# The layer-norm transposes move from TensorE and PSUM to transposing DMAs on the sync engine's queue

## The reference

```
x = x + 0.5 * ffn(layernorm(x))
x = x + attn(layernorm(x))
x = x + 0.5 * ffn(layernorm(x))

attn: q, k, v = x@Wq+bq, x@Wk+bk, x@Wv+bv       # 16 query heads, 4 key/value heads, head size 64
      out = softmax(causal(q/8 @ k.T)) @ v
      out = layernorm(out)*ln_g + ln_b ; return out @ Wo + bo

ffn:  cluster_scores = x @ cluster_sigs.T ; tile_scores = x @ sigs.T     # 8 + 64 columns
      tile_idx = best of 8 tiles in the best of 8 clusters (spline-calibrated gates)
      comp = tanh(gelu(x@w1 + b1) @ w2 + b2)                             # 1024 -> 256 -> 2
      mag  = relu(comp @ spline_w1[tile_idx] + ...) @ spline_w2[tile_idx] + ...
      return layernorm(x + mag * directions[tile_idx] * output_scale) * gamma + beta
```

## Time and profile before

| | us |
|---|---|
| median of 9 runs | 1154.55 (1151.77 to 1174.88) |
| the profiled execution | 1154.83 |
| its span, slowest core (7) | 1153.3 |
| spans of the other cores | 1141.0 to 1148.3 |

### The profile page before, as it was taken

The page is one execution under the profiler, slowest core; times in us unless marked ns, Lnnn a source line. Parts: engine busy times, 40 slices in busy tenths (PEclk is TensorE's granted clock), DMA queues, the critical chain, the costliest instruction groups (busy, mean ns, idle before and its releaser), DMA issues.

```text
span 1153.3 us, 12663 instructions; the slowest of 8 cores (1141.0 to 1153.3 us)
## 1 busy us (share of the span) xinstructions
PE 809.7 (70%) x3804; PEld 322.3 (28%) x3804; DVE 482.8 (42%) x921; ACT 508.7 (44%) x489; POOL 14.2 (1%) x22
## 2 busy tenths in 40 slices
PE   2067663595999556757778878888469958766097
PEld 1043211233444312312222222222143325311032
DVE  1851833686200274453342233121445554570643
ACT  0061332003332454548879999989770024233100
POOL 0100000000000000000000000000000010000000
PEclk9999955555799756559979999999759976855555
DMA  5800000005200040000000000000000030000034
GB/s 142 201 2 0 1 0 1 0 1 76 35 1 1 4 70 1 1 1 1 1 1 1 1 1 1 1 1 1 1 1 1 1 33 1 0 1 0 0 127 166
DMA packets 23903, 25.25 MB, mean 22 GB/s; under 512 B 13209, under 2 KB 17562, under 8 KB 23840
## 3 DMA queue, kind: packets, MB, share of 16 engines
q0 software_dynamic: 12240, 7.09, 4.8%
q1 hardware_dynamic: 11600, 17.34, 4.5%
HBM read 23.13 MB, written 8.39 MB: 27 GB/s over the span
## 4 chain that ended last, share of the span: by engine, by line
PE 50%; ACT 22%; DVE 16%; issue 9%; SPq 1%; DVEq 1%; DMA 0%; ACTq 0%
ACT sE L1405 12%; PE pQ L943 7%; PE pO L1184 5%; PE pW L1335 5%; PE pS L1246 4%; PE pTR L362 4%; ACT sXFB L1405 4%; PE pH L626 3%; DVE sSTAT L1405 3%; ACT sHH L1405 3%; PE pD L857 3%; PE pD L846 3%; PE pD L851 3%; PE pM L700 3%; PE pS L679 2%
## 5 line engine op out<-in xcount | busy, mean ns | idle before, releaser
L1405 ACT ACTIVATE sE<-pS,sNB 128x1024 bf16<-128x1024 f32 (+1 forms) x320 | 297.5, 991 | 72.5 <-PE pS L1246 70.4
L1184 PE MATMUL pO<-sE,sVTM 128*65 128x512 bf16 (+3 forms) x640 | 196.8, 393 | 24.2 <-DVE sTMPA L1405 22.4
L1246 PE MATMUL pS<-sQT,sKT 64*128 64x512 bf16 (+3 forms) x640 | 125.3, 383 | 54.1 <-DVE sE L1405 33.9
L362 PE MATMUL pTR<-sIDB,sXFB 128*128 128x128 bf16 x512 | 75.2, 265 | 82.6 <-ACT sXFB L1405 80.8
L1405 DVE TENSOR_TENSOR sE<-sE,sTRI 128x256 bf16<-128x256 bf16 x128 | 36.9, 291 | 156.2 <-ACT sE L1405 155.7
L1246 PEld LDWEIGHTS pS<-sQT,sKT 64*128 64x128 bf16 x640 | 36.6, 94 | 174.2 <-issue 172.0
L362 PEld LDWEIGHTS pTR<-sIDB,sXFB 128*128 128x128 bf16 x512 | 53.2, 104 | 106.4 <-issue 94.0
L1184 PEld LDWEIGHTS pO<-sE,sVTM 128*65 128x65 bf16 x640 | 47.6, 116 | 97.8 <-issue 92.7
L1405 ACT ACTIVATE sRS<-sSCR 128x16 f32<-128x16 f32 x6 | 1.4, 229 | 166.0 <-DVE sSCR L1405 165.9
L1405 DVE COPY sT<-pTR 128x1024 bf16<-128x1024 bf16 x64 | 44.2, 691 | 49.0 <-PE pTR L362 49.0
L1405 DVE BATCH_NORM_STATS2 sSTAT<-sX 128x6 f32<-128x512 f32 x96 | 60.3, 682 | 9.4 <-ACT sGB L1405 6.1
(11 more groups left out here) (177 smaller groups left out, 833.3 us busy)
## 6 DMA issues: line engine op xcount, KB each, us to landing
sX<-x SPq DMA_DIRECT2D x4, 2048.0 KB, 20.9
y<-sX SPq DMA_DIRECT2D x16, 512.0 KB, 2.6
sWQ<-wq POOLq DMA_DIRECT2D x1, 2048.0 KB, 17.5
sWO<-wo POOLq DMA_DIRECT2D x1, 2048.0 KB, 15.4
sW1C<-cw POOLq DMA_DIRECT2D x2, 512.0 KB, 10.1
sWK<-wk POOLq DMA_DIRECT2D x1, 512.0 KB, 19.3
sWV<-wv POOLq DMA_DIRECT2D x1, 512.0 KB, 21.1
sSGR<-sigsT SPq DMA_DIRECT2D x1, 256.0 KB, 16.2
```

Source lines behind the costliest of these rows:

```text
L362: tt.transpose(pTR[:, par3, c, :], sXFB[:, par, 128 * c:128 * (c + 1)], sIDB[:]),
L1184: mi = t.matmul(pO[:, h, lv:512], sVTM[:, c, gg, :], sE[:, epar, h, lv:512], start=(c == 0), stop=(c == cmax - 1))
L1246: mi = t.matmul(pS[:, cpar, h, lv:512], sKT[o:o + 64, kchunk, 128 * c:128 * (c + 1)], sQT[o:o + 64, hp, q0:qe], start=True, stop=True, til ...
L1405: self._last = a(*args, **kw)
```

## The change

The PSUM buffers `pTR`, the 512 PE transposes and the 64 DVE copies go. For each tile SP issues one transposing DMA that reads the 128x1024 tile in `sXFB` and writes `sT[:, 0:8, 128t:128t+128]` directly. Each tile gets a semaphore of its own, `LNT0` to `LNT15`, raised by 16 when the DMA has landed; it takes the place of both old marks, so ACT's tile t now waits until the DMA of tile t-2 has landed, and PE's matmuls wait for the DMAs of the tiles they read. Two waits are added or spelled out because of it: the `psc` groups and the first `pQ` wait for every tile's own semaphore, and ACT's `sDSQ` waits for `tern`, whose scratch memory it reuses.

```diff
     def emit_ln_transpose(stack, src_tiles, rs, aux_ready, src3d=False):
-        pTR = psum(stack, "pTR", [128, 3, NC, 128], BF16)
...
             lns = P.mark("s", "LNS")
-            par3 = t % 3
-            for c in range(NC):
-                wt = [lns]
-                if t >= 3 and c == 0:
-                    wt.append(lnv_hist[t - 3])
-                P.st("t", lambda tt, par=par, par3=par3, c=c:
-                     tt.transpose(pTR[:, par3, c, :], sXFB[:, par, 128 * c:128 * (c + 1)],
-                                  sIDB[:]),
-                     wait=wt)
-            lnt_hist.append(P.mark("t", "LNT"))
-            P.st("v", lambda v, t=t, par3=par3:
-                 v.tensor_copy(sT[:, 0:NC, 128 * t:128 * (t + 1)], pTR[:, par3]),
-                 wait=[lnt_hist[-1]])
-            lnv_hist.append(P.mark("v", "LNV"))
+            sem = f"LNT{t}"
+            P.new_sem(sem)
+            P.st("y", lambda e, t=t, par=par: e.dma_start_transpose(
+                     out=sT[:, 0:NC, 128 * t:128 * (t + 1)], in_=sXFB[:, par, :]),
+                 wait=[lns], inc=[(sem, 16)])
+            tup = (sem, P.val[sem])
+            lnt_hist.append(tup)
+            lnv_hist.append(tup)
         return lnv_hist
...
-            P.mark("v", "AUX")
+            tern_m = P.mark("v", "AUX")
...
             P.st("s", lambda s: s.activation(sDSQ[:], sDIR[:], AF.Square),
-                 wait=[ldg_d])
+                 wait=[ldg_d, tern_m])
...
-            P.st("t", f, wait=[lnv[4 * s4 + 3]])
+            P.st("t", f, wait=[lnv[4 * s4], lnv[4 * s4 + 1], lnv[4 * s4 + 2],
+                               lnv[4 * s4 + 3]])
...
-            w = [ldg_qkv, lnv2[NT - 1]] if ji == 0 else []
+            w = ([ldg_qkv] + list(lnv2)) if ji == 0 else []
```

## The result

The changed kernel is slower: the median of ten runs is 1191.45 us (1188.53 to 1209.66), against 1154.67 us for the kernel before. The ratio is 1.0321 with an interval of 1.0304 to 1.0337.

The account below looks back on a forecast made before the run. No engine was taken to bound everything; in the four stages touched, ACT was nearly the bound. 18.3 + 38.2 - 17.5 + 25.1 = +64.1 us on 1154.83 gave 1219 us, range 1145 to 1500, likeliest 1160 to 1290.

Parts of the forecast that it names:

- A: First stage, from its first ACT tile to the start of `psc`: +18.3 us.
- B: Projection stage, from its first ACT tile to `pQ`: +21.4 us for landings, +16.8 for weight loads, together +38.2.
- D: Last stage, ACT to the end of `psc`, and `pdt`: +17.9, +1.7 for `pdt`, +5.5 for loads, together +25.1 us.
- P: Period of a pair of tiles with two buffers, one ACT tile plus L plus two wake-ups: 5.56 us.
- L: Latency of a transposing DMA from issue to landing: 4.02 us, 1.30 fixed and 2.72 for 64 pieces an engine.
- C: Output projection stage, ACT to the end of `pW`: `pW` starts after tile 0's landing, the rest hides behind PE, -17.5 us.
- the two terms for the loads: Loads that don't fit between the transposes on the DMA engines: +16.8 us in B, +5.5 in D.
- Plain-copy pace: Rival: a transposition moves like a plain copy of 2 KB rows, L = 1.88, 1145 us; chance 0.10 (below 1152).
- Blocks in series: Rival: eight 128x128 blocks one after another per tile, L = 14.4, 1501 us; above 1500 0.11, shared with the write side.
- the write side: Rival: 32-byte written pieces set the price, 21.8 us a tile, 2391 us; above 1500 0.11, shared with Blocks in series.
- No overlap in C: Rival: `pW` waits for more than its tile, costing 17.5 + 22, 1259 us; inside the likeliest range, no chance of its own.
- One DMA at a time in the queue: Case for all stages: transposing DMAs run singly, last landing at 65.9 us, 1255 us; no chance of its own.

Follow-up runs that it names:

- The halves: Changed kernel with each tile moved by two transposing DMAs of 128x512 in place of one of 128x1024: 1206.48 us, one run.
- the piece experiment: Kernel before plus twelve lone 256 KB DMAs during the projections (2 KB rows, 256-byte pieces from SBUF or HBM, transposing): 1156.24 us, one run.

## Why the prediction was right, point by point

- **The mechanism held.** ACT's tiles wait for landings in A, B and D, with P = ACT + L + two wake-ups. The sign follows, and the experiment with four buffers shows in A that it is latency: the same DMAs, the same landing time, and no loss. One sign that the prediction had named failed: in A, C and D the DMA engines are not nearly full (mean shares 0.58, 0.63 and 0.71), since a tile's transfer is cheaper than it had held.
- **The size of L was off**: 3.2 against 4.02, and by the prediction's own 24 us for each us of L that is 20 of the 27 us that were too many; the rest are the two terms for the loads, 3.8 in B and about 5 in D. That L missed by no more than 0.82 is partly luck, since two errors of opposite sign met in it. Of the two parts of L, the pieces were too dear and the rest too cheap. In C, q1's packets took 0.594 x 16 x 36 us / 14785 = 23.1 ns each, so 66 of them are 1.52 us, not 2.72; the rest of L is then 1.7, not 1.30. The halves agree: 33 x 23.1 ns + 1.7 = 2.5 us, which is what they took. The count of pieces was nearly right (66 for 64), but their price came from another queue in a nearly full window, and the piece experiment shows that it doesn't hold for a lone DMA.

  The window of C, 886 to 922 us:

```profile
q1 hardware_dynamic: 14785, 3.67, 59.4%
```

- **A**: with the measured L, the predicted +18.3 becomes 18.3 - 7 x 0.82 = +12.6, which is what was measured. `psc` hangs on ACT's last tile and the sums, as said.
- **B**: the latency term, 21.4 - 8 x 0.82 = 14.8, stands beside 14.1 measured by the kernel with early weights (its B against before's). The term for the loads was 16.8 and is 13.0. I had treated the DMA engines as a shared amount of work, spread over the stage. In fact nearly all of it falls on the first pair, with a landing of up to 17.1 us, and later pairs run at their own pace. The trace shows why: while both queues had work, the engines took their packets one for one, 1950 and 1950 in 12 us. So a tile's 66 small packets on an engine waited for about 66 larger ones of the weights. Two tiles at 89 ns a packet are 11.7 us, an estimate from this window, near the 13.0 measured.
- **C**: right to 0.2 us, with some luck: with the measured L the sum would have been -17.5 - 0.8 = -18.3, and `pW` itself took 71.1 us instead of 70.44. And the reason was told too simply. The order of the instructions gives about 11.5 us of it by itself.
- **D**: 17.9 - 8 x 0.82 = 11.3 for the latency, 11.8 measured; so the loads cost about 0.5 on core 3, not 5.5. On cores 4 and 5, where ACT waited 5.35 and 4.60 us for the first landing, D took 2 to 3 us longer. The +1.7 of `pdt` came as said on most cores; on core 3 its stretch was granted 0.81 where before it was granted 1.00. But the row behind it was a lucky one: before, `pdt` in A took 8.6 us or more on three cores, among them the one that was read, and 7.07 on the other five behind the same sparse matmuls.
- **The rivals.** Plain-copy pace (L = 1.88) fell, but less far off than I held: plain 2 KB rows between SBUF addresses need 2.4 us, so by the prediction's sum even a transposing DMA at that pace would have stood just above the break-even of 2.28. Blocks in series (14.4) and the write side (21.8) fell at the first landing. No overlap in C fell: `pW` waits once. One DMA at a time in the queue is refuted by the kernel with four buffers.

## What to carry to other kernels

A transposition by DMA in place of TensorE swaps work beside the path for a latency on it: count the buffers before you count the busy time. A buffer is taken while it is written, in flight and noticed, here 1.24 + 3.2 + 0.2 = 4.7 us; divided by the period of a tile, 1.38, that is 3.4, and four buffers sufficed in A where two did not (three were not run). Look at what shares the DMA engines in that stretch, and count packets and not only bytes, because here small packets took turns one for one with the larger ones of a weight load. And when such a change speeds a stage up, try the new order with the old operation: here two thirds of C's gain was order.

## What the runs showed that I had not expected

- SP is taken for 1.218 us by a transposing DMA, whether of 1024 columns or 512, and for 0.505 us by a plain one of 2 KB rows. With four buffers a tile left every 1.38 us in A. DMA engines are also nearly full in that stretch (share 0.99), so which of the two is the ceiling there is open; with the halves it is SP.

  The kernel with four buffers, window of stage A:

```profile
61.00:82.00 21.00, 0.00 (x0) 0.00 (x0) 1.25 (x5) 18.22 (x16) 0.00 (x0) 1.00 0.99 181
```

- Eight transposes on TensorE among dense matmuls at granted 1.00 add 0.45 us, 56 ns each, where they took 1.17 us at granted 0.50 between waits, as two tiles' sixteen took 2.36 before. By the single durations it would be 8 x 0.266 = 2.13: a transpose's own duration, start to end, doesn't say what it costs in a pipelined row.
